# Trainium2 transformer layer: the down projection of one token group emitted ahead of the next group's quantization

## The reference, cut to what matters

```python
def _weight_quant(w):      # ternary: -1, 0, 1 times one scale
    scale = 1.0 / jnp.clip(jnp.mean(jnp.abs(w)), 1e-05)
    wq = jnp.clip(jnp.round(w * scale), -1.0, 1.0) / scale
    return w + jax.lax.stop_gradient(wq - w)
def _act_quant(x):         # 8 bit, one scale per token
    scale = 127.0 / jnp.clip(jnp.max(jnp.abs(x), axis=-1, keepdims=True), 1e-05)
    xq = jnp.clip(jnp.round(x * scale), -128.0, 127.0) / scale
    return x + jax.lax.stop_gradient(xq - x)
def _bitlinear(x, w):
    return jnp.einsum('bsi,oi->bso', _act_quant(x), _weight_quant(w))
# layer 0
x = x + attention(_layernorm(x))
xn = _layernorm(x)
gate = jax.nn.silu(_bitlinear(xn, w_gate))
up = _bitlinear(xn, w_up)
x = x + _bitlinear(gate * up, w_down)
```

## Time and profile before

| | us |
|---|---|
| median of 3 runs | 3328.2 (3325.19 to 3362.68) |
| the profiled execution | 3336.96 |
| its span, slowest core (core 5) | 3335.3 |
| spans of the 8 cores | 3296.2 to 3335.3 |
| PE busy in the span | 1317.9 (40%) |
| DVE busy in the span | 1426.4 (43%) |
| feed-forward stage, from the first transpose of `xq_fm` to the end | 2017.6 to 3335.3 |

### The profile page before, as it was taken

One profiled execution on the slowest core, in us unless ns is written; L12 is line 12 of the kernel. 1 busy time (PEld: TensorE's weight loads), 2 busy tenths in 40 slices (PEclk: granted clock), 3 DMA queues, 4 the chain that ended last, 5 costly groups with the idle time before them and its releaser, 6 DMA issues. The chain is left out here.

```text
span 3335.3 us, 22659 instructions; the slowest of 8 cores (3296.2 to 3335.3 us)
## 1 busy us (share of the span) xinstructions
PE 1317.9 (40%) x5952; PEld 605.4 (18%) x5952; DVE 1426.4 (43%) x1946; ACT 433.4 (13%) x787; POOL 47.1 (1%) x84
## 2 busy tenths in 40 slices
PE   0000247263414333242334032929237914953307
PEld 0000123021202112121212021404113401421103
DVE  3334034454475754445466752282252226233401
ACT  2210000131220213222211110101000100110000
POOL 1000000000000000000000000000000000000000
PEclk9999978685757666666667565969678957986758
DMA  4435632541113121211122245524355436644526
GB/s 123 123 102 150 104 82 48 145 136 45 62 58 111 55 84 53 66 48 60 45 85 85 60 122 136 153 79 147 102 161 191 141 85 198 189 131 140 191 47 202
DMA packets 312315, 362.28 MB, mean 109 GB/s; under 512 B 117625, under 2 KB 207740, under 8 KB 312188
## 3 DMA queue, kind: packets, MB, share of 16 engines
q1 hardware_dynamic: 253292, 218.17, 23.5%
q10 hardware_dynamic: 47104, 109.06, 10.3%
q0 software_dynamic: 11792, 33.60, 3.6%
HBM read 276.91 MB, written 67.11 MB: 103 GB/s over the span
## 5 line engine op out<-in xcount | busy, mean ns | idle before, releaser
L919 PE MATMUL psF<-Wbuf,k_fm 128*128 128x512 bf16 x1024 | 253.3, 412 | 474.9 <-DMA k_fm<-scr_kh 328.9
L643 PE MATMUL psT<-eye_bf,P_sb 128*128 128x128 bf16 x256 | 65.3, 268 | 656.9 <-ACT P_sb L625 577.8
L824 PE MATMUL psF<-Wbuf,xq_fm 128*128 128x512 bf16 x1024 | 246.4, 384 | 99.7 <-DMA Wbuf<-scr_tg 99.7
L834 PE MATMUL psF<-Wbuf,xq_fm 128*128 128x512 bf16 x1024 | 248.1, 386 | 79.0 <-DVE h_grp L848 68.9
L848 DVE SCALAR_TENSOR_TENSOR h_grp<-psF,sclu,sg_sb 128x512 f32<-128x512 f32 x128 | 96.1, 751 | 390.7 <-PE psF L834 381.5
L482 PE MATMUL psA<-xn_fm,Wbuf 128*128 128x512 bf16 x256 | 63.8, 394 | 458.2 <-DMA xn_fm<-scr_xn 393.7
L323 DVE TENSOR_TENSOR wacc<-wacc,wabs 128x512 f32<-128x512 f32 x192 | 132.8, 692 | 221.0 <-ACT wabs L319 214.9
L919 PEld LDWEIGHTS psF<-Wbuf,k_fm 128*128 128x128 bf16 x1024 | 105.3, 104 | 622.9 <-issue 524.0
L387 DVE TENSOR_SCALAR Wmk<-Wstg,cthr 128x512 bf16<-128x512 f32 x192 | 93.0, 485 | 247.1 <-DMA Wstg<-wgT 102.6
L844 ACT ACTIVATE sg_sb<-psF,sclg 128x512 f32<-128x512 f32 x128 | 87.9, 687 | 810.4 <-PE psF L824 736.1
L282 DVE SCALAR_TENSOR_TENSOR kq<-h_grp,qr 128x2048 bf16<-128x2048 f32 x32 | 73.4, 2292 | 223.0 <-DMA scr_kh<-kq 219.3
(11 more groups left out here) (111 smaller groups left out, 1557.0 us busy)
## 6 DMA issues: line engine op xcount, KB each, us to landing
Wbuf<-scr_td ACTq DMA_DIRECT2D x32, 2048.0 KB, 11.3
Wstg<-wgT SPq DMA_DIRECT2D x128, 256.0 KB, 3.1
Wstg<-wuT SPq DMA_DIRECT2D x128, 256.0 KB, 3.0
Wstg<-wdT SPq DMA_DIRECT2D x128, 256.0 KB, 2.9
Wbuf<-scr_tg SPq DMA_DIRECT2D x32, 1024.0 KB, 7.0
Wbuf<-scr_tu SPq DMA_DIRECT2D x32, 1024.0 KB, 8.3
x_sb<-x ACTq DMA_DIRECT2D x32, 512.0 KB, 4.9
scr_kh<-kq POOLq DMA_DIRECT2D x32, 512.0 KB, 3.8
```

The lines of the kernel that those rows point to most:

```text
L643: tok = p.run("pe", lambda e, kc=kc, pp=pp: e.transpose(psT[kc % 2][:, :], P_sb[pp][:, kc * 128:(kc + 1) * 128], eye_bf[:, :]), reads=[pb, ...
L824: tok = p.run("pe", lambda e, ic=ic, c=c, bg=bg, goff=goff: e.matmul(bg[:, :], xq_fm[:, ic * S + c * 128: ic * S + c * 128 + 128], Wbuf[0] ...
L834: tok = p.run("pe", lambda e, ic=ic, c=c, bu=bu, goff=goff: e.matmul(bu[:, :], xq_fm[:, ic * S + c * 128: ic * S + c * 128 + 128], Wbuf[1] ...
L919: tok = p.run("pe", lambda e, cc=cc, oh=oh, jc=jc, ic=ic, bi=bi, ib=ib, wdst=wdst: e.matmul(psF[bi][:, :], k_fm[:, ic * 512 + cc * 128: ic ...
```

## The change

In the loop over the groups the call `emit_down(g - 1)` moves ahead of `emit_quant(g)`. Nothing else is edited; for g = 0 and behind the loop the order stays as it was.

```diff
         for g in range(N_GRP):
             emit_gateup(g)
             if g >= 1:
                 emit_kfm(g - 1)
+                emit_down(g - 1)
             emit_quant(g)
-            if g >= 1:
-                emit_down(g - 1)
         emit_kfm(N_GRP - 1)
         emit_down(N_GRP - 1)
```

## The result

| | before | after |
|---|---|---|
| median of 10 runs, us | 3332.69 (3320.23 to 3362.68) | 3441.59 (3417.67 to 3466.52) |
| ratio after / before | | 1.0331 (95% interval 1.029 to 1.0372) |
| profiled execution: span of the slowest core, us | 3335.3 (core 5) | 3431.0 (core 4) |
| PE busy, DVE busy, us | 1317.9, 1426.4 | 1322.4, 1426.5 |

A forecast was written before the change was run, and what follows sets the result against it. It took the feed-forward stage to be steps waiting for each other, with no engine full. Losses of 37.5 + 37.7 + 42.1 = 117.3 us on the median 3328.2 us gave 3446 us; range 3425 to 3480 us.

The forecast's parts named there:

- Down projection, undisturbed: Down projection of a group with no quantization beside it: 81.36 us from T to the end of the last L943.
- T: The moment at which PE starts a group's down projection, when its 32 transposes are through.
- Quantization, undisturbed: DVE's quantization of a group, now behind the last L943 and unable to overlap the down projection: 75.88 us.
- Rival C: Quantization disturbed by the first weight slices, last transposes gain nothing: 152 us of loss, 3480 us; chance 12%.
- Five sets of gate/up ahead: During quantization PE does five sets of 8 matmuls until its banks are full; resumption to third set takes 6.32 us.
- The mark: Start of the third gate/up set after PE resumes, chunk 3's L834, where PE runs evenly in both kernels.
- Rival A: PE runs on through the quantization in gate/up without slowdown: 20 us less, 3308 us, within 2%; chance 3%.
- DVE works in strict order: DVE's queue is first-in first-out, so L848 of the next gate/up stage waits behind the quantization.
- Group 3: Its last transposes start 52.6 us later, behind the quantization's last store, but run 10.5 us shorter: net 42.1 us.
- rival B: Quantization on no path, not even ahead of the last transposes: -106 us, 3222 us, faster; chance 1%.
- the two middle terms: Later arrival at the mark from group 1 to 2, 37.5 us, and from group 2 to 3, 37.7 us.

The follow-up runs named there:

- interleaved run: Against the kernel before: quantization cut in two pairs of chunks, each pair placed ahead of one half of the down projection; 3271.02 us, ratio 0.9836.
- the fastest version: Kernel before plus store/transpose row tracking split by group, transposes not waiting for each other, and quantization pairs alternating with down projection halves; 3065.07 us, ratio 0.9224.
- the rows apart in the old order: Kernel before with the rows of `scr_kh` tracked by group, so quantization stores don't wait for the preceding group's transposes; 3250.06 us, ratio 0.9749.

## Why the prediction was right

The forecast was 3446 us and 117 us of loss; measured were 3441.6 us and some 110 us. The time is closer than the loss by luck: the loss was put 7 us too high, and the median that it was added to, 3328.2 us of three runs, was 4.5 us below that of ten. Step by step, on the slowest core of the changed kernel and over all cores:

- **Down projection, undisturbed, 81.4 us.** From T to the end of the last L943 it took 84.0 us in group 0 (2410.88 to 2494.89) and 81.0 in group 1 (2754.93 to 2835.89). Right to 3 us.
- **Quantization, undisturbed, 75.9 us, with nothing hidden.** 75.06 us in group 1, 0.8 us below what I had called the least. The waits for `kq` are 0.3 us in all, so the reason for taking the lower bound held: hardly any load was beside it. Rival C falls. The interleaved run shows that the figure depends on this: there a pair took 48.3 us and not 37.5.
- **Five sets of gate/up ahead, restart in 6.3 us.** Five sets, and 2576.66 - 2570.75 = 5.9 us. The mark came 165.8 us after T, expected were 164.5. Rival A falls: PE did not get beyond its banks.
- **DVE works in strict order.** DVE took no later instruction first: PE had ended the set that L848 reads at about 2499, and L848 started at 2569.86, right behind the quantization. The Trainium skill, "PSUM — Partial Sum Buffer", section "Engine vs sequencer instructions", gives strict first-in first-out order as the rule for this queue. The trace agrees.
- **Group 3.** The first transpose came 164.2 us after T (expected 161.7), and not at PE's end some 76 us after T, so rival B falls. The last set took 83.7 to 91.7 us over the cores, median 85.1 (expected 84.3), against 93.8 to 100.5 before, median 95.0: the gain of 10 us without weight loads beside them was real. T(2) to T(3), on my figures 203.9 + 42.1 = 246.0 us, is 246.7 in the median.

What was a little off is the size of the two middle terms, 37.5 and 37.7 us. They are 34.1 and 31.1 us in the medians of the cores. I had read the times before from core 5 alone, whose stretch from T(1) to T(2) was 301.9 us where the median of the cores was 306.2. Up to the first L848, the part that the prediction added up, the medians grew by 36.8 and 35.5 us, close to the forecast. What took some of it back is the stretch from there to the next T, which became 3 us shorter (186.0 to 183.1); the last down projection did too (79.5 to 76.3). No experiment separates these from the difference between executions: with g = 3 alone, where these two groups keep the old order, the stretch is 185.0 and 183.7 us.

What the prediction said nothing of is that both kernels lie well above what the same work allows: the fastest version took 3065 us. It took the transposes as fixed and the wait of the stores for them as given. The runs put the price of that wait at 84 us and that of the transposes' waits for each other at another 160 us or so (ratio 0.9749 to 0.9273).

## What to carry to other kernels

A wait that a reorder removes is worth only what lies behind it: look at what the instruction that used to fill the wait will now stand in front of, and under what work it will run. Here 33.6 us of idle TensorE came off between the halves, and 76 us of VectorE work came onto the path, of which the next stage could cover only what its PSUM banks hold. Cutting the filler into pieces that fit the gaps, or removing a false dependency so that it starts earlier, gained where moving it whole lost.

Before reordering, check which of the waits in the chain are made by the dependency tracking alone. One name for a whole DRAM tensor or for a whole tile of transposes cost this kernel some 240 us, twice the 110 us that the new order lost or the 115 us that the kernel without the three quantizations gained.

## What the runs showed of the hardware that I had not expected

- DMA transposes of 512 x 128 bf16 issued on one queue without waiting for each other took 40.8 to 42.2 us for 32, 1.3 us each, with only two output stores beside them (last set of the fastest version), and 51.5 to 57.9 us beside weight loads and stores of `kq`. One by one they took 2.6 us each when nothing else was in flight.
- The same transposes one by one, beside eight stores of 512 KB, took 106.6 to 116.3 us for 32, and 98.5 to 107.0 us without the stores (the kernel before, and the one without the quantization in the old order).
- The mean granted clock of TensorE was 0.740 to 0.750 over the cores of the kernel before, 0.738 to 0.743 in the changed one and 0.769 to 0.773 in the fastest. It does not follow the time alone: with the rows apart in the old order, 84 us faster than before, it was 0.742 to 0.747.
